# Rotary products and squares over q and k in one instruction each, in a fused attention and feed-forward kernel

## What is computed

```
h = shift_token(x)
qkv = h @ wqkv                      # 128 -> 3 x 512
q, k, v = split(qkv, 3)             # 8 heads of 64 each
q = l2norm(q) * qs
k = l2norm(k) * ksc
q, k = rotary_xpos(q, k)            # q*cos*scale + rotate_half(q)*sin*scale, k with 1/scale
o = local_attention(q, k, v)        # windows of 64, each looks one back
x = x + o @ wo
h = layernorm(shift_token(x)) * lg + lb
a, g = split(h @ w1 + b1, 2)
x = x + (a * gelu(g)) @ w2 + b2
```

## Time and profile before

| | |
|---|---|
| median of 3 runs | 510.57 us (510.19 to 510.65) |
| profiled execution, span from first to last instruction | 509.7 us |
| PE matmul busy | 400.0 us (78%) |
| DVE busy | 421.6 us (83%) |
| ACT busy | 306.6 us (60%) |
| POOL busy | 191.7 us (38%) |
| L1004, the rotation's products, 128 instructions | 87.1 us |
| L809, the squares, 64 instructions | 36.9 us |
| mean granted clock of TensorE | 0.912 of full |

### The profile page before, as it was taken

How to read it: one execution, slowest core, us unless ns; L and a number is a source line. 1 busy time by engine, 2 the same in 40 slices (tenths; PEclk the granted TensorE clock), 3 DMA queues, 4 the chain that set the end, 5 groups by cost and what they waited for, 6 DMA issues and landing times.

```text
span 509.7 us, 11479 instructions
## 1 busy us (share of the span) xinstructions
PE 400.0 (78%) x3768; PEld 325.1 (64%) x3768; DVE 421.6 (83%) x1071; ACT 306.6 (60%) x884; POOL 191.7 (38%) x159
## 2 busy tenths in 40 slices
PE   2641068999998999899989998999897889787552
PEld 1330046777776877687768776877686678576432
DVE  6788968999999799969996999799778997874544
ACT  2363067686767766676768576777575677465120
POOL 2016735454645254515441454244423542330000
PEclk9795577999999999899989999999897999799856
DMA  8400241211421042105111411141114210120100
GB/s 281 132 0 0 62 105 42 73 27 31 111 61 28 18 124 50 26 18 128 47 29 35 123 36 28 48 120 28 28 27 114 51 26 15 31 49 1 22 21 21
DMA packets 42401, 28.22 MB, mean 55 GB/s; under 512 B 21700, under 2 KB 36598, under 8 KB 42358
## 3 DMA queue, kind: packets, MB, share of 16 engines
q1 hardware_dynamic: 42357, 27.68, 20.8%
HBM read 13.51 MB, written 3.15 MB: 33 GB/s over the span
## 4 chain that ended last, share of the span: by engine, by line
PE 50%; DVE 31%; issue 12%; ACT 4%; POOL 1%; DMA 1%; DVEq 1%; POOLq 0%; ACTq 0%
PE upper L624 10%; PE bank L513 5%; PE upper L602 4%; PE bank L517 4%; PE bank L514 4%; PE upper L608 4%; DVE h L1029 4%; PE bank L673 4%; PE bank L638 4%; PE upper L619 3%; DVE ss L1010 3%; DVE rn L856 2%; ACT probs L788 2%; DVE rot_sin L1004 2%; DVE neg_max L1051 2%
## 5 line engine op out<-in xcount | busy, mean ns | idle before, releaser
L788 ACT ACTIVATE probs<-upper,neg_max 128x128 f32<-128x128 f32 x256 | 90.4, 368 | 77.0 <-DVE neg_max L1051 75.1
L477 POOL TENSOR_TENSOR rot<-rot_cos,rot_sin 128x512 f32<-128x512 f32 x32 | 40.8, 1274 | 149.4 <-PE upper L573 143.0
L486 POOL TENSOR_TENSOR rot<-rot,rn 128x1024 f32<-128x1024 f32 x32 | 63.3, 1978 | 73.5 <-DVE rn L881 71.5
L513 PE MATMUL bank<-wqkv_hi,act_t_hi 128*128 128x512 f32 x96 | 43.1, 449 | 16.5 <-DVE o_tok L1061 8.5
L624 PE MATMUL upper<-k_t,q_even 128*64 128x128 f32 x512 | 56.0, 299 | 0.0
L788 ACT ACTIVATION_READ_ACCUMULATOR probs<-upper,neg_max 128x1 f32 x256 | 52.9, 206 | 0.0
L624 PE MATMUL upper<-k_t,q_odd 128*64 128x128 f32 x512 | 52.5, 286 | 0.0
L1051 DVE TENSOR_REDUCE neg_max<-upper 128x4 f32<-128x512 f32 x64 | 43.1, 682 | 4.4 <-PE upper L624 3.5
L1004 DVE TENSOR_TENSOR rot_cos<-bank,tab 128x512 f32<-128x512 f32 x64 | 43.6, 681 | 2.2 <-PE bank L517 2.2
L1010 DVE TENSOR_REDUCE ss<-sq 128x16 f32<-128x1024 f32 x32 | 38.8, 1212 | 5.7 <-ACT sq L809 5.5
L1004 DVE TENSOR_TENSOR rot_sin<-bank,tab 128x512 f32<-128x512 f32 x64 | 43.5, 679 | 0.0
(11 more groups left out here) (128 smaller groups left out, 1004.5 us busy)
## 6 DMA issues: line engine op xcount, KB each, us to landing
v_mid<-v_tok SPq DMA_DIRECT2D x64, 128.0 KB, 2.3
tab_raw<-tables SPq DMA_DIRECT2D x8, 512.0 KB, 3.5
h_tok<-group_in SPq DMA_DIRECT2D x14, 128.0 KB, 3.5
x_res<-group_in SPq DMA_DIRECT2D x28, 64.0 KB, 1.8
wqkv_raw<-wqkv SPq DMA_DIRECT2D x2, 768.0 KB, 6.5
x_in<-x SPq DMA_DIRECT2D x4, 256.0 KB, 3.7
head_scale<-head_scales SPq DMA_DIRECT2D x8, 128.0 KB, 3.7
group_in<-normed SPq DMA_DIRECT2D x4, 256.0 KB
```

Of the source, the lines that this page charges most:

```text
L486: pool.tensor_tensor(rot[:, :, :], rot[:, :, :], rn[:, 0:2 * HEADS].unsqueeze(2).broadcast_to([P, 2 * HEADS, DH]), ALU.mult).then_inc(rot_ ...
L513: pe.matmul(out_ap, lhs, rhs, start=True, stop=False)
L788: last = act.activation(probs[:, h, :], s_bank[half][:, (h % 4) * P:(h % 4 + 1) * P], ACT.Exp, bias=neg_max[a.par][:, h:h + 1], accum_out= ...
```

## The change

The PSUM banks 0 to 3 become one tensor, `lower`, and `qk_banks` is its view of banks 0 and 1 together. `rotate` waits for `q_done` and `k_done` and then issues two products of 1024 columns, cosine and sine, each over q and k; the table is read with a step over its q and k parts. ACT issues one square of 1024 columns behind both. The semaphores `q_rot` and `k_rot` become `qk_rot`, two counts a tile, and `squared` has one count a tile.

```
-        bank = [ctx.enter_context(nc.psum_tensor(f"bank{i}", [P, 512], F32)) for i in range(4)]
+        lower = ctx.enter_context(nc.psum_tensor("lower", [P, 4, 512], F32))
+        bank = [lower[:, i, :] for i in range(4)]
...
+        qk_banks = lower[:, 0:2, :]
...
-                        pool.wait_ge(q_rot, 2 * (t + 1))
-                        pool.wait_ge(k_rot, 2 * (t + 1))
+                        pool.wait_ge(qk_rot, 2 * (t + 1))
...
-                need(pe, q_rot, 2 * a.t)
-                need(pe, k_rot, 2 * a.t)
-                need(pe, squared, 2 * a.t)
+                need(pe, qk_rot, 2 * a.t)
+                need(pe, squared, a.t)
...
-                        for n, (b, read) in enumerate(((q_bank, q_rot), (k_bank, k_rot))):
-                            act.wait_ge(read, 2 * (cur.t + 1))
-                            act.activation(sq[:, n * INNER:(n + 1) * INNER], b[:, :], ACT.Square).then_inc(squared, 1)
+                        act.wait_ge(qk_rot, 2 * (cur.t + 1))
+                        act.activation(sq[:, :].rearrange("p (n f) -> p n f", n=2), qk_banks, ACT.Square).then_inc(squared, 1)
...
-                for n, (b, ready, done) in enumerate(((q_bank, q_done, q_rot), (k_bank, k_done, k_rot))):
-                    dve.wait_ge(ready, a.t + 1)
-                    src = b[:, :].rearrange("p (h d) -> p h d", h=HEADS)
-                    for m, dst in enumerate((rot_cos, rot_sin)):
-                        table = tab[:, a.slot, (2 * n + m) * DH:(2 * n + m + 1) * DH]
-                        dve.tensor_tensor(dst[:, n * HEADS:(n + 1) * HEADS, :], src,
-                                          table.unsqueeze(1).broadcast_to([P, HEADS, DH]), ALU.mult).then_inc(done, 1)
+                dve.wait_ge(q_done, a.t + 1)
+                dve.wait_ge(k_done, a.t + 1)
+                src = qk_banks.rearrange("p n (h d) -> p n h d", h=HEADS)
+                tables_of = tab[:, a.slot, :].rearrange("p (n m d) -> p n m d", n=2, m=2)
+                for m, dst in enumerate((rot_cos, rot_sin)):
+                    table = tables_of[:, :, m, :].unsqueeze(2).broadcast_to([P, 2, HEADS, DH])
+                    dve.tensor_tensor(dst[:, :, :].rearrange("p (n h) d -> p n h d", n=2), src, table,
+                                      ALU.mult).then_inc(qk_rot, 1)
...
-                dve.wait_ge(squared, 2 * (a.t + 1))
+                dve.wait_ge(squared, a.t + 1)
```

More of the change, by code:

```diff
@@ L197, in sandwich_kernel @@
         q_done, k_done, v_done = sem("q_done"), sem("k_done"), sem("v_done")
-        q_rot, k_rot, squared, rn_ready = sem("q_rot"), sem("k_rot"), sem("squared"), sem("rn_ready")
+        qk_rot, squared, rn_ready = sem("qk_rot"), sem("squared"), sem("rn_ready")
         rot_added, rot_scaled = sem("rot_added"), sem("rot_scaled")
@@ L653, in feed_forward @@
                     if c == 1:
-                        pe.wait_ge(q_rot, 2 * taken)
-                        pe.wait_ge(k_rot, 2 * taken)
-                        pe.wait_ge(squared, 2 * taken)
+                        pe.wait_ge(qk_rot, 2 * taken)
+                        pe.wait_ge(squared, taken)
                     if c == 2:
```

## The result

The changed kernel takes 522.81 us (median of 4 runs, 517.91 to 523.05), the kernel before 510.61 in the same comparison. The ratio is 1.020, with an interval of 1.017 to 1.024. It is slower, as forecast, but by more: the medians differ by 12.2 where 6.0 was forecast, and the median lies 1.3 above the upper end of the range. The ratio gives less, 10.4 (8.7 to 12.0), because the four runs don't lie together: one took 517.91, the other three 522.7 to 523.1. The profiled execution has a span of 521.2 (509.7 before).

A forecast was written before the change was run, and what follows sets the result against it. It took two near-equal loops, DVE's own queue and the path through ACT and PE, to bound steps 0 and 1; 3.0 + 1.6 + 3.9 + 0.5 + 0.4 - 3.4 gave 6.0 more, median 516.6, range 508.5 to 521.5.

The forecast's parts named there:

- the two loops of nearly the same length: In steps 0 and 1, DVE's own queue and the loop through all other engines; k ready 0.01 before DVE.
- steps 0 and 1: First two of a four-tile pass's four steps, rotation to rotation; forecast about 10.50 long, where they lasted 10.18 and 10.21.
- the path through PE: Rotation, squares, ACT's copies, scores, next tile's k: 10.17 from rotation to next k, forecast to become 10.47.
- Rivals 1, 2 and 3: 1: faster by the port, 508.7, chance 0.17; 2: path alone, 516.8 or 513.4, 0.20; 3: DVE bound, 506.4, 0.05.
- Rival 4: Dearer instructions (rotations of twice 0.68 add 5.4), or no fall of the clock goes: 520 to 522, chance 0.13.
- Rotation and square: Rotations end 2.34 behind rotation start R; one square of 1.02 ends at R + 3.40, 0.30 later than before.
- The start behind k: In steps 0 and 1, the rotation was taken to come 0.03 behind the end of k.
- The held clamp: DVE instruction behind the sum of squares, held by POOL's addition: 0.9 longer in step 1; six steps 1 cost 3.9.
- Step 3: Last step of a pass: rotation starts 0.43 later, covered by DVE's 10.57 to the next rotation.
- The clock: TensorE's clock falls behind PE's wait for h2, 1.7 each; two of three expected to go, -3.4.
- The first four tiles: Rotation there starts before k is done; the wait for k, POOL and the later square cost 3.0.
- h2 and for the clamp in step 3: Early h2 of the last group but one lost, 0.5; held instruction in step 3, half of four cases, 0.4.

The follow-up runs named there:

- the kernel with h2 first and no clamp: Kernel before, h2 normalised ahead of the probs_t copy in step 2, and clamp and scaling behind the sum of squares removed: 495.69, ratio 0.968.
- The kernel without the clamp: Changed kernel without the clamp and scaling instruction behind the sum of squares (square takes a factor, sum negated, floor left out): 515.53, ratio 1.009.
- the wait alone: Kernel before, its small instructions kept, but the rotation waits for k as well as q before its first product: 516.30, ratio 1.009.
- h2 first: Kernel before, with the normalising of h2 moved ahead of the probs_t copy in step 2: 502.81, ratio 0.982.
- the change with h2 first: Changed kernel, with the normalising of h2 moved ahead of the probs_t copy in step 2: 513.46, ratio 1.002.
- the square alone: Kernel before, with only the squares merged into one of 1024 columns behind all four products: 512.66, ratio 1.002.

## Where the prediction was right, and where not

The direction held, and so did the mechanism of the change: k late in front of the rotation, and each tenth between the rotation and the next k coming out again. What was wrong in the picture of the kernel before are the two loops of nearly the same length in steps 0 and 1. There DVE's queue alone set the step, as the 9.97 of the kernel with h2 first and no clamp shows; it is the wait for k that gives the path through PE its hold on the step. Rivals 1, 2 and 3 are out: k came late in front of most rotations, and the clamp did not slip in before POOL. Rival 4 has the nearest time, 520 to 522, but not the reason: the instructions were not dearer, and one fall of the clock went. Term by term:

**Rotation and square** were right to 0.01: 2.34, 1.02 to 1.03, the sum at R + 3.44. The next k, forecast at R + 10.47, comes at R + 10.45 to 10.56 in steps 0 and 1.

**The start behind k was mis-sized.** The sum took 0.03, read off rotations that weren't waiting for k at all: DVE came from its own queue at the moment at which k was done. Where DVE truly stands waiting for PE, it starts 0.14 behind. A step that the path decides lasts 10.46 + 0.14 = 10.60 and not 10.50, in some passes 10.67. Over the six passes steps 0 cost 3.1; five of 0.32 were forecast.

**The held clamp** was right for step 1 (11.0 there, 10.7 to 11.2 measured), but, chiefly by the 0.11 more of delay, in steps 0, 1 and 3 it mostly came 0.07 to 0.16 behind the end of the first addition, and not 0.05 ahead of it. It is held either way. All steps 1 together cost 4.5 over six passes and another 0.8 in the last one, against 3.9: seven steps of 0.76 where six of 0.65 were forecast. The kernel without the clamp shows both parts: 10.6 to 10.7 by the path alone, the remainder by the hold.

**Step 3 was covered, or nearly.** Forecast was that its rotation may start 0.43 later at no cost, since the next one doesn't move. One pass of the changed kernel, from step 2 to the next step 0, beside 305.07, 323.20 and 333.77 in the earlier trace rows, and the k ahead of that step 0:

```profile
312.91 1.22 DVE L1003 TENSOR_TENSOR rot_cos<-lower,tab 128x1024 f32<-128x1024 f32 x1
...
331.47 1.23 DVE L1003 TENSOR_TENSOR rot_cos<-lower,tab 128x1024 f32<-128x1024 f32 x1 [0.47 <-PE lower L518]
...
341.68 1.23 DVE L1003 TENSOR_TENSOR rot_cos<-lower,tab 128x1024 f32<-128x1024 f32 x1
```

```profile
341.15 0.40 PE L518 MATMUL lower<-wqkv_lo,act_t_hi 128*128 128x512 f32 x1
```

The rotation starts 0.14 behind k instead of 0.4 before it, and this step 2 lasts 18.56 instead of 18.13. Step 3 gives nearly all of it back, 10.21 instead of 10.57; the two together are 28.77, before 28.70. The other group without a fall of the clock in either kernel has 29.09 and 28.96. With the wait alone the two steps are even 0.8 shorter over six passes, its extra fall (1.6) taken out. In the change they are 0.8 longer, the fall that went taken out, 0.7 of it in the last of the six passes. The reason given in the prediction held less well: the path through PE did not come out before the next rotation. In this pass and in two others it is k that decides it (341.55, 0.13 ahead).

**The clock.** The count was wrong: one of three falls in the loop went, not two. Steps 2 with a fall last 20.14 and without one 18.55, 1.6 a fall (1.7 estimated). -3.4 should have been -1.6. Two windows of the changed kernel, to be read as the earlier trace rows:

```profile
267.00:270.00 3.00, 2.38 (x15) 1.78 (x17) 2.69 (x9) 1.38 (x2) 0.39 (x1) 0.63 0.00 0
369.00:372.00 3.00, 2.03 (x13) 1.44 (x15) 2.83 (x8) 1.35 (x3) 0.73 (x2) 0.70 0.02 3
```

PE's wait for h2 did become shorter (9.6 in total, against 11.5 in the earlier trace rows, longest 1.6), as the text argued, but two falls stayed, and that the third went for this reason isn't shown. These are events of single executions: one run of the four took 517.91 at a mean granted clock of 0.936, the other three 522.7 to 523.1 at 0.917 to 0.924.

**The first four tiles and the end.** 3.0 was forecast up to the fourth rotation and 3.0 came, but the agreement to a tenth proves little. Up to tile 3 h2 isn't normalised yet, so moving that can't matter there; still the fourth rotation starts at 93.0 in the kernel before and 94.2 with h2 first, at 96.0 in the change and 97.1 in the change with h2 first. Single executions differ there by 1. What does hold is the difference between the kinds of kernel: in the seven whose rotation waits for k the fourth rotation starts at 95.4 to 97.1, in the four in which it doesn't at 92.0 to 94.7. Behind tile 27 another 1.8 was lost, for which the sum had only part of its steps 0 and 1.

Of the 5.5 between 6.0 and 11.5 (the difference of the spans), 1.8 are the clock, 1.5 steps 0, 1.4 steps 1 with the last one, and the remaining 0.8 is what steps 2 and 3 lost otherwise and the end, less the 0.9 that the sum had for h2 and for the clamp in step 3. How this last part splits over its causes stays open.

**What the change really trades** shows in the runs that take it apart. The wait for k takes 4.4 by itself. The later square costs 3.0 in steps 0 and 1, and a gain at h2 covers it; whether that would stay so with h2 first wasn't run. In steps 0 and 1 the parts nearly add up, 2.7 for the wait, 3.0 for the square and 1.8 that go with the clamp, 7.5 of 7.6, though the square alone ended 0.19 later than in the change. The medians don't add up, 4.4 and 0.8 against 12.2, since h2 and the clock come out differently in each kernel. The shorter instructions of DVE bring nothing where the path decides, because DVE then waits in front of the next rotation.

The fastest kernel that computes all that the reference asks is the one with h2 first, at 502.81, 1.8% under the kernel before.

## What to carry to other kernels

Merging two instructions is not only a saving on their engine: it delays the first half's start to the second operand's arrival, and the first half's end to the second half's end. Count what each consumer loses before counting the overhead saved, and check whether one of the two halves had been running ahead of its producer. To price a new wait, take the start behind a producer only from rows where the consumer was really idle; a row in which it happens to arrive at the same time says nothing of it. And when two queues seem equally long, remove something from one of them and see whether the step shortens.

## What of the hardware was unexpected

- DVE starts 0.14 behind the modelled end of the matmul for which it waits, 0.20 in the kernel where another wait stands behind the decisive one. ACT starts 0.04 behind DVE.
- Reading across two PSUM banks has no extra price: 1.22 and 1.21 for products of 1024 columns, 1.03 for the square, against 0.68 and 0.60 for 512.
- How late the clamp comes during POOL's additions decides by hundredths: begun 0.12 before the end of the first it took 0.17, 0.05 before it 1.30, 0.10 behind it 1.17. In the change this one instruction of 128x16 is busy for 25.0, where 32 times its free 0.17 are 5.4.
- Not every DVE instruction is held: the sum of squares at 203.08 ran right under POOL's addition from 202.97 and took 1.22, its mean over the whole kernel.
